# Attention probabilities turned by transposing DMAs through HBM for 22 of 32 head pairs, with weighings and loads in new places

## The reference, cut to what matters

```
Q = einsum('btc,ncd->btnd', x, W_Q) + b_Q      # and K, V; Q and K are then rotated (rope)
scores = einsum('bqnd,bknd->bnqk', Q, K) / math.sqrt(d_head)
scores = where(causal, scores, -inf)
probs = softmax(scores, axis=-1)
z = einsum('bnqk,bknd->bqnd', probs, V)
out = einsum('bqnd,ndm->bqm', z, W_O) + b_O
```

## Time and profile before

| | us |
|---|---|
| median of 3 runs | 954.27 (952.92 to 955.51) |
| the profiled execution: its time | 953.62 |
| the profiled execution: its span | 951.8 |
| TensorE busy | 911.5 |
| VectorE busy | 778.2 |
| GpSimd busy | 503.2 |
| ScalarE busy | 438.8 |

### The profile page before, as it was taken

One profiled execution on the slowest core, in us unless ns is written; L12 is line 12 of the kernel. 1 busy time (PEld: TensorE's weight loads), 2 busy tenths in 40 slices (PEclk: granted clock), 3 DMA queues, 4 the chain that ended last, 5 costly groups with the idle time before them and its releaser, 6 DMA issues.

```text
span 951.8 us, 19467 instructions
## 1 busy us (share of the span) xinstructions
PE 911.5 (96%) x6305; PEld 818.4 (86%) x6305; DVE 778.2 (82%) x1704; ACT 438.8 (46%) x1227; POOL 503.2 (53%) x380
## 2 busy tenths in 40 slices
PE   7899999999999999999999999989998799999996
PEld 6798888989899888998888888877887699999985
DVE  6988877977887999877799877767779688888867
ACT  3656655454334663333564333462156244444431
POOL 1433424465453436776354677525617377777760
PEclk9999999999999999999999999999999899999999
DMA  7796399899157952303793221315151277777768
GB/s 270 252 364 227 131 320 389 313 395 362 46 182 250 401 208 89 112 25 123 292 370 113 91 110 55 120 62 237 60 209 69 69 130 127 131 130 127 134 115 311
DMA packets 75584, 179.08 MB, mean 188 GB/s; under 512 B 7776, under 2 KB 42464, under 8 KB 74464
## 3 DMA queue, kind: packets, MB, share of 16 engines
q1 hardware_dynamic: 61040, 158.80, 46.0%
q0 software_dynamic: 14448, 19.05, 12.1%
HBM read 98.35 MB, written 79.47 MB: 187 GB/s over the span
## 4 chain that ended last, share of the span: by engine, by line
PE 80%; DVE 7%; issue 5%; POOL 3%; ACT 2%; DMA 1%; SPq 0%; DVEq 0%; ACTq 0%
PE bank L550 11%; PE bank L552 10%; PE bank L551 10%; PE bank L854 6%; PE bank L632 6%; PE bank L956 4%; POOL xs L1352 3%; PE bank L832 3%; PE bank L834 3%; PE bank L836 3%; PE bank L618 3%; PE bank L658 3%; PE bank L660 3%; PE bank L659 3%; PE bank L914 2%
## 5 line engine op out<-in xcount | busy, mean ns | idle before, releaser
L1312 POOL TENSOR_TENSOR z_lo<-prob_t,z_hi 128x512 fp32r<-128x512 f32 x64 | 82.5, 1297 | 188.5 <-ACT z_hi L1199 169.4
L1516 DVE SCALAR_TENSOR_TENSOR turn<-bank,bqk,trig 128x1024 f32<-128x1024 f32 x128 | 160.6, 1276 | 23.3 <-PE bank L552 20.8
L1344 POOL TENSOR_TENSOR rot<-turn 128x512 f32<-128x512 f32 x64 | 96.0, 1500 | 110.0 <-DVE turn L1516 94.6
L1405 POOL DMA_INDIRECT sums<-ysb,token_at x79 | 123.3, 1561 | 56.6 <-DMA sums<-ysb,token_at 28.0
L550 PE MATMUL bank<-xt_hi,w_hi 128*128 128x512 f32 x256 | 105.7, 413 | 3.4 <-DVE xt_lo L1480 1.7
L1185 ACT COPY prob_t<-bank 128x512 f32<-128x512 f32 x64 | 37.5, 586 | 148.8 <-PE bank L618 142.1
L1144 ACT ACTIVATE prob<-prob,negmax 128x128 f32<-128x128 f32 x256 | 99.1, 389 | 2.5 <-DVE negmax L1501 2.4
L552 PE MATMUL bank<-xt_hi,w_lo 128*128 128x512 f32 x256 | 100.1, 391 | 0.0
L551 PE MATMUL bank<-xt_lo,w_hi 128*128 128x512 f32 x256 | 99.7, 390 | 0.0
L1352 POOL DMA_INDIRECT xs<-xh,dest x64 | 74.3, 1161 | 41.2 <-issue 37.4
L1155 ACT COPY v<-bank 128x512 f32<-128x512 f32 x64 | 37.6, 587 | 114.5 <-PE bank L552 113.5
(11 more groups left out here) (197 smaller groups left out, 2643.3 us busy)
## 6 DMA issues: line engine op xcount, KB each, us to landing
xs<-zeros SPq DMA_DIRECT2D x16, 2120.0 KB, 15.3
w_hi<-w_dram SPq DMA_DIRECT2D x24, 768.0 KB, 9.7
w_lo<-w_dram SPq DMA_DIRECT2D x24, 768.0 KB, 9.1
xe_all<-xs SPq DMA_DIRECT2D x79, 132.5 KB
wo_hi<-wo_dram SPq DMA_DIRECT2D x26, 256.0 KB, 9.1
wo_lo<-wo_dram SPq DMA_DIRECT2D x26, 256.0 KB, 10.1
sums<-zeros SPq DMA_DIRECT2D x3, 2176.0 KB, 12.8
raw<-in_wqkv SPq DMA_DIRECT2D x16, 384.0 KB, 4.5
```

The lines of the kernel that those rows point to most:

```text
L1344: nc.gpsimd.tensor_tensor(rot[m][1][:], turn[m][1], turn[m][2], ALU.add).then_inc(rot_pool, 1)
L1405: nc.gpsimd.indirect_dma_start(sums_dram[s % SUMS], bass.IndirectOffsetOnAxis(ap=token_at[:, s:s + 1], axis=0), ysb[s % YBUFS][:], None, c ...
L1516: last = nc.vector.scalar_tensor_tensor(turn_all[m][:, 2 * i:2 * i + 2, :], qk_bank[2 * m + i][:].unsqueeze(1).to_broadcast([128, 2, GT]), ...
```

## The change

For the pairs t = 8 to 29 (`by_dma(t)`), which are weighed in steps 10 to 31, TensorE no longer turns the probabilities. ScalarE splits each head's fp32 probabilities into two planes of 16 bits (`prob_planes`), SP stores the planes to HBM (`prob_store`, 256 KB in rows of 256 bytes), waits for that store, and a transposing DMA brings them back as `prob_t` (`prob_turn`, 256 KB). The copies L1185 of these pairs are gone too. The other ten pairs stay as they were.

In these steps the weighings move: head 0 is weighed after projection QE (after the scores where p is 0 or 3), head 1 after KE. The loads of the weights go one pair ahead and stand between stores and turns on SP, and the zero fills and the fills of `sums` get other steps. On ScalarE the exponentials of head 0 now stand ahead of the taking of weighing 0, those of head 1 between the two; on VectorE the scaling of head 1's probabilities stands ahead of the two `rot`; on GpSimd the scaling of head 0's stands ahead of both `rot`, and `z_lo` of head 1 between them. At p = 1 and 2 both halves of the values come first. The turns of the mixer's output (p = 0) and the router's turns and logits (p = 2) move within their steps. Six semaphores are merged into others, which leaves their waits where they were.

```diff
@@ -69,8 +69,20 @@
 PARTS_DOWN = EXPERTS // GB
 
 
-FILL_STEPS = ([(1, p) for p in range(4)] + [(1, p) for p in (4, 4, 5, 5, 6, 6, 7)] + [(2, 3)]
-              + [(2, 3)] + [(GROUPS - 1, p) for p in (2, 3, 3)])
+FILL_STEPS = ([(1, p) for p in (0, 0, 1, 1)] + [(1, p) for p in (2, 3, 4, 4)] + [(1, p) for p in (5, 5, 6, 6)]
+              + [(1, 7)] + [(2, p) for p in (1, 2, 3)])
+
+
+def by_dma(t):
+    return PAIRS <= t < PAIRS * GROUPS - 2
+
+
+def dma_before(t):
+    return min(max(t - PAIRS, 0), PAIRS * (GROUPS - 1) - 2)
+
+
+def pe_before(t):
+    return t - dma_before(t)
...
+            def prob_store(t, h):
+                sp.wait_ge(planes_ready, 2 * dma_before(t) + h + 1)
+                rows = prob_dram[t % 2, h].rearrange("(b q i) k -> q b i k", b=GB, i=2)
+                sp.dma_start(rows, planes[h][:]).then_inc(prob_stored, 16)
+
+            def prob_turn(t, h):
+                sp.wait_ge(prob_stored, 16 * (2 * dma_before(t) + h + 1))
+                sp.wait_ge(z_lo_done, 2 * (t - 1) + h + 1)
+                sp.dma_start_transpose(prob_t[h][:].rearrange("p b q -> p (b q)").unsqueeze(1).bitcast(U16),
+                                       prob_dram[t % 2, h]).then_inc(prob_landed[h], 16)
+
...
             for g in range(1, GROUPS):
                 for p in range(PAIRS):
-                    at = W_AT[p]
-                    if g == 1 and W_NTH[p] == 0:
-                        sp.wait_ge(w_stored[at], 64 * W_USES[at])
-                    sp.wait_ge(v_ready, 2 * (PAIRS * (g - 1) + W_BEFORE[p] + 1))
-                    sp.wait_ge(wo_done, PAIRS * (g - 1) + W_BEFORE[p] - 1)
+                    t = g * PAIRS + p - 2
+                    if by_dma(t):
+                        prob_store(t, 0)
+                    if 0 < p < PAIRS - 1:
+                        load_w(g, p + 1)
+                    if by_dma(t):
+                        prob_turn(t, 0)
+                        prob_store(t, 1)
+                    if 0 < p < PAIRS - 1:
+                        load_o(g, p + 1)
+                    if by_dma(t):
+                        prob_turn(t, 1)
+                    if p == 0:
+                        load_w(g, 1)
+                        load_o(g, 1)
+                    if p == PAIRS - 1 and g < GROUPS - 1:
+                        load_w(g + 1, 0)
+                        load_o(g + 1, 0)
                     if g > 1 and p == 3:
                         sp.wait_ge(y_taken, FILTERS * (g - 1))
                         sp.dma_start(c_t[:], ctxt_in[g - 1]).then_inc(ctxt_loaded, 16)
-                    sp.dma_start(w_hi[:, at].bitcast(F32), w_dram[p, 0]).then_inc(w_loaded[at], 16)
-                    sp.dma_start(w_lo[:, at].bitcast(F32), w_dram[p, 1]).then_inc(w_loaded[at], 16)
-                    load_wo(p)
                     for n, at_step in enumerate(FILL_STEPS):
                         if at_step == (g, p):
                             fill(n // PARTS, n % PARTS)
...
 
             def weigh_values(s, p, h, first):
 
-                pe.wait_ge(pt_taken, s * 2 - 4 + h + 1)
+                t = s - 2
+                if by_dma(t):
+                    pe.wait_ge(prob_landed[h], 16 * (dma_before(t) + 1))
+                    if h == 0:
+                        pe.wait_ge(v_taken, s * 2 - 2)
+                else:
+                    pe.wait_ge(pt_taken, 2 * pe_before(t) + h + 1)
                 if not (first and p == 2 and h == 0):
                     pe.wait_ge(zt_taken, s * 2 - 4 + h)
...
+                h = g - 1
+                if p == 2 and 1 < g < GROUPS:
+                    two_banks_free(g, p, live)
+                    pe.wait_ge(v_taken, s * 2 - 1)
+                    token_turn(h - 1)
...
+                if p == 0 and 1 < g < GROUPS:
+                    two_banks_free(g, p, live)
+                    pe.wait_ge(v_taken, s * 2 - 1)
+                    cross_back(h - 1)
                 beside_first(g, p, live)
-                if live(2):
+                by_pe = live(2) and not by_dma(s - 2)
+                if by_pe:
                     transpose_probs(s, 0, live, order)
...
-                if live(2):
+                if by_pe:
                     transpose_probs(s, 1, live, order)
                     weigh_values(s, p, 0, first)
                     between_weighings(g, p, live)
@@ -864,6 +924,13 @@
                     if live(1) and order == (1, 0):
                         project_values(0)
                     weigh_values(s, p, 1, first)
+                elif live(2):
+                    between_weighings(g, p, live)
+                    if p in (0, 3):
+                        weigh_values(s, p, 0, first)
+                    if p == 2 and g > 1:
+                        pe.wait_ge(v_taken, s * 2)
+                        token_logits(g - 2, pt_bank)
                 beside_second(g, p, live)
...
                         project(p, col, qk_bank[i][:]).then_inc(qk_ready, 1)
-                if p == 2 and g > 1 and live(0):
-                    pe.wait_ge(zt_taken, s * 2 - 2)
-                    token_logits(g - 2, zt_bank)
+                    if live(2) and not by_pe and i == 0 and p not in (0, 3):
+                        weigh_values(s, p, 0, first)
+                    if live(2) and not by_pe and i == 2:
+                        weigh_values(s, p, 1, first)
...
+            def prob_planes(t, h):
+                act.wait_ge(prob_ready[h], t + 1)
+                if dma_before(t):
+                    act.wait_ge(prob_stored, 16 * (2 * dma_before(t) + h - 1))
+                nc.scalar.copy(planes[h][:], prob[h][:].bitcast(U16).rearrange("p b (k i) -> p b i k", i=2)).then_inc(planes_ready, 1)
...
+                if by_dma(s - 2):
+                    prob_planes(s - 2, 1)
...
+                if by_dma(s - 2):
+                    if p == 3:
+                        take_turned(v_t, g - 1, vt_ready, vt_taken)
+                    for h in range(2):
+                        exps(h)
+                        take_weighed(h)
+                        weighed_high(h)
+                elif live(2):
...
-                if live(1):
+                if live(1) and not by_dma(s - 2):
                     exps(0)
                     exps(1)
+                if by_dma(s - 1):
+                    prob_planes(s - 1, 0)
...
             def core_step(g, p, live, first):
                 s = g * PAIRS + p
+                late = by_dma(s - 2)
                 if live(2):
-                    z_low(g, p, live)
+                    z_low(s, 0)
+                    if not late:
+                        z_low(s, 1)
+                if late:
+                    first_probs(s)
                 for m in range(2):
+                    if late and m:
+                        z_low(s, 1)
                     if live(0):
                         pool.wait_ge(qk_used, s * 4 + 2 * m + 2)
                         if live(1):
                             pool.wait_ge(s_ready, s * 2)
                         pool_rot(m, s)
-                    if m == 0 and live(1):
-
-                        pool.wait_ge(rtotal_ready, s * 2 - 1)
-                        nc.gpsimd.tensor_tensor(prob[0][:], prob[0][:],
-                                                rtotal[:, 0, :].unsqueeze(2).to_broadcast([128, GB, SEQ]),
-                                                ALU.mult).then_inc(prob_ready[0], 1)
...
-                        if h == 1 and live(2):
-                            dve.wait_ge(pt_ready, s * 2 - 2)
+                        if by_dma(s - 2):
+                            dve.wait_ge(planes_ready, 2 * dma_before(s - 2) + h + 1)
...
+                def second_probs():
+                    dve.wait_ge(rtotal_ready, s * 2)
+                    nc.vector.tensor_tensor(prob[1][:], prob[1][:],
+                                            rtotal[:, 1, :].unsqueeze(2).to_broadcast([128, GB, SEQ]),
+                                            ALU.mult).then_inc(prob_ready[1], 1)
+
+                if by_dma(s - 1):
+                    second_probs()
...
-                if live(1):
-                    dve.wait_ge(rtotal_ready, s * 2)
-                    nc.vector.tensor_tensor(prob[1][:], prob[1][:],
-                                            rtotal[:, 1, :].unsqueeze(2).to_broadcast([128, GB, SEQ]),
-                                            ALU.mult).then_inc(prob_ready[1], 1)
+                if live(1) and not by_dma(s - 1):
...
                         tokens_low(h - 1)
+                    if p == 0:
+                        cross_add(h - 1)
                     if p == 3:
...
             def beside_scored(g, p, live):
                 h = g - 1
-                if p == 0 and h > 0:
+                if p == 2 and h > 0 and live(0):
+                    logits_take(h - 1, pt_bank)
+                if p == 0 and g == GROUPS:
```

134 lines of the change are left out of this document (74 added, 60 removed).

## The result

The changed kernel takes **959.75 us**, median of 20 runs (955.57 to 966.96), beside 955.85 us for the kernel before (20 runs): ratio 1.0045, interval 1.0025 to 1.0065. In a later series of runs the same two kernels stood at 960.34 and 951.00: ratio 1.0123 (1.0089 to 1.0157). The forecast was 6 us faster; it is slower, by 0.5% or by 1.2%. The profiled execution took 957.1 us.

A forecast was written before the change was run, and what follows sets the result against it. TensorE was taken to bound the kernel; turns removed and old waits gone, less new waits, late turns and 3.3 us for fills, gave 6.0 us off the profiled 953.62: 947.6, as a median 948; range 934 to 980.

The forecast's parts named there:

- Steps with p = 4 to 7: Twelve steps where a wait replaces the turns: 21.2 us against 21.44, 3 us gained for the twelve.
- The wait that takes the turns' place: Filter 4 waits 1.0 us for VectorE's product of filter 2, until S + 3.6; S ends the scores' issue.
- old waits for ScalarE: A weighing's waits for ScalarE's taking of the one before, 3.2 us; 2.3 of it was to go.
- the double fills: Steps 12 to 14 issue two fills each; turn 1 lands late in steps 14 and 15, 3.3 us lost.
- rival (c): Filter 4 doesn't wait, VectorE's product coming by S + 2.6: 1.0 us more in 12 steps, 936; chance 0.11.
- Steps with p = 0 to 3: Ten steps without that filter: the turns' 1.02 us come off each, less new waits for ScalarE and late turns.
- At p = 0 no loads stand between (free): At p = 0 the turns land in time, costing nothing; 2 x 1.0 us gained.
- x: Data time of one transposing DMA: taken as 1.2 us, bounds 0.75 and 3.4; turn 0 lands T + 8.5 + x, T the step's start.
- Rival (a): Transposing DMA slow, both weighings wait: at x = 3.4, 38 us more, 986; decides from x = 1.6; chance 0.28.
- likeliest case: The sum as worked out, x from 0.75 to 1.45: 944 to 952 us, chance 0.42.
- VectorE ... 3.5 us ahead: Scaling of head 1 (1.55 us) ahead of `rot` costs nothing: `rot` ended 3.5 us before the scores, 1.4 cover stays.
- Rival (b): Transposing DMA goes block by block, x = 16.4, every step bound by it: about 1,550 us; chance 0.06.

The follow-up runs named there:

- the last experiment: Changed kernel, turned by DMA only in the twelve steps with p = 4 to 7, weighing 0 there between filters 3 and 4: 948.21 us, 0.9964.
- the side-by-side runs: Unaltered changed kernel beside it with step 15's fill moved to step 31, and the kernel before: 960.34 us (1.0123), 953.79 (1.0035), 951.00.

## Why the prediction was wrong

**Steps with p = 4 to 7: the mechanism right, the sum near by luck.** The wait that takes the turns' place, its releaser, S + 3.5 and 21.3 us were as forecast. The twelve steps came out at -1.5 us, forecast -2.0, but by two errors that offset each other. Of the 5.3 us of gains (3.0 and 2.3) only some 2.4 came: step 22 with its 21.44 us was taken for all, while steps 12 to 15 had taken 21.21 before and so gained nothing, and of the 3.2 us of old waits for ScalarE only 1.1 lay in these steps, 1.8 with one that the trace puts down to "issue" (0.87 lay ahead of step 10, 1.26 behind step 31). And of the 3.3 us that the double fills were to lose only 0.9 came, in step 14. What rival (c) would be worth the last experiment shows: without that wait a step takes 20.5 us.

**Steps with p = 0 to 3: wrong, and the sign with them.** Forecast 4.0 us less, measured 7.4 more. The steps of the working that failed:

1. *"At p = 0 no loads stand between (free)" and "The fills ... 3.3 in all".* The queue was followed to step 15's own turns and not to the store of step 16, ahead of which stood step 15's loads for the next group and its fill. p = 0 missed by 4.7 us: step 16 by 5.6, while step 24 came out 1.0 better than forecast. Shown: with that one fill elsewhere step 16 falls by 5.1 us and the kernel is 0.9% faster, and the same fills without stores cost nothing that shows.
2. *"I take 1.2" for x, and 4.5 us for the loads.* x is 1.3 to 1.6 us in a quiet queue, not 1.2 (20 ns for a packet of 256 bytes where 16 were taken), and more where the turn runs into the end of loads: half of the 44 turns took over 1.6 us and eleven over 2, 2.3 in step 10, 2.8 at most, which the text had named as a sign of being wrong. The loads of 1.5 MB took 5.7 us in step 10, not 4.5 (4.7 to 7.2 over steps 10 to 31). In step 10 weighing 0 started at T + 11.4 and weighing 1 at T + 16.4, forecast 9.7 and 13.5 for their turns; the p = 1 steps and step 10 together missed by 2.1 us. Rival (a) gave x = 1.6 as the point from which it decides, and that is where the middle of the 44 turns lies (1.66). x lies between the bounds of 0.75 and 3.4 but for the most part above the 0.75 to 1.45 of the likeliest case.
3. *"VectorE ... 3.5 us ahead", costing nothing.* That cover was read in step 22 and taken for all. In steps 10 and 18 the scores now wait for `rot` (0.95 and 1.16 us; the waits for `rot` that the text had named as a sign of being wrong), and steps 18 and 26 missed by 1.7 us; at p = 3 the second projection of step 19 waits for VectorE (1.9 us), and turn 0 was late besides, in step 27 by 2.4, which missed 2.8. The run without turns keeps the wait for `rot` in step 10 and has that for `vcs` in both steps 19 and 27 (1.9 us each), so the turns are not their cause. The wait for `rot` in step 18 is gone there, and in the second execution of the changed kernel too, so that one comes and goes. What share the scaling's new place, the logits' new place and slower rots have was not separated.
4. *Not in the sum at all: the clock.* The text priced a wait at its length. Of the 10.9 us of the side-by-side runs up to 5.5 are low clock. In the profile of the kernel before, steps 10 to 31 have none. Waits do not all bring it: in two profiled executions of the changed kernel it fell after those of 3.48 and 3.41 us in step 16 and 3.04 in step 27; after 2.0 to 2.7 us it fell sometimes (2.03 in step 19 of the second execution, yes, in the row below; 2.41 in step 27 of the first and 2.73 in step 10 with the fill moved, no).

```profile
355.80:359.30 3.50, 3.50 (x10) 1.95 (x8) 3.17 (x6) 2.15 (x9) 0.00 (x0) 0.51 0.48 121
```

**The rules of the Trainium skill's pages.** Rival (b), blocks one by one, is out: a whole head is turned in about 1.5 us of DMA time, not ten. So the 1309 ns for one block in the Trainium skill's page "VectorE: DVE Perf Modes", section "The three transpose paths", do not add up over eight blocks here; that page's rule, TensorE where PSUM will do, still came out right for the ten steps with p = 0 to 3. What the Trainium skill's page "Advanced Engine Details and Errata", section "X-Bar Transpose (TRN2)", says, that transposing DMAs are as fast as regular ones, the trace bears out only roughly, and in a quiet queue only: 1.3 to 1.6 us for a turn against 1.0 to 1.2 for the store of the same bytes.

**What stays open.** In the run without turns the profile gains 5.6 us in steps 10 to 31 and the medians about 1. The two profiles are of different series, and between these the kernel before itself moved, from 955.85 to 950.8 us; it was profiled in the first alone. Within the series the mean clock, 0.9915 against 0.9926, is worth 1.0 us of the rest. And what stands behind step 31 took 346.4 us before, 347.9 without turns, 349.4 in the last experiment (whose steps gain 7.4 us and whose median gains 3.4; it opens with a wait of 2.44 us for `z_lo`) and 342.7 to 349.4 over the profiles at hand (nearly the same code in all). How much of a gain in the steps is given back there, and why, was not found. Nor was it settled why the changed kernel lost 0.5% in one series and 1.2% in another.

## What to carry to other kernels

Where a small transfer on the critical path shares a queue with large ones, write down what stands ahead of it at every step boundary, the step after a fill too, and do not answer with a queue of its own before measuring: packets of 256 bytes beside packets of 4 KB were four times slower than behind them, and their DMA six. TensorE paid for new waits of 2.0 to 3.5 us once as idle time and often again as half clock, so work taken off a full TensorE has to be worth more than its waits look. And look for cover in the fullest step of the other engines, not in a typical one: the turns paid only in the four of eight steps in which they were not waited for, and there only once the work of a weighing filled the wait for VectorE that they had left behind. Last, a row read in one step stands for its kind only after the other steps have been read too: step 22 stood for twelve steps and for VectorE's cover, and both times wrongly.

## What the runs showed of the hardware that was not expected

- A turn of a head (256 KB read, 1024 packets of 256 bytes) takes 1.3 to 1.6 us of data time in a quiet queue and up to 2.8 among the ends of loads in its own. Two beside loads and a fill on another queue took 17.8 us, beside loads alone 9.3 and 11.3, and with nothing beside them 3.8.
- SyncE is held 1.16 us by the issue of a transposing DMA, against mostly 0.39 to 0.58 for a store, and for up to 2.06 us in some of the 44.
- The store's rows went out as 512 packets of 512 bytes, mostly 26 to 30 ns each, not as 1024 of 256.
- VectorE's `rot` took 1562 ns by the mean of steps 10 to 31 instead of 1221, and the scaling of head 1 1090 instead of 1455, after the two changed places. In the changed kernel a `rot` took 0.68 us with no instruction of GpSimd beside it and 1.55 us or more with one beside it in all but one case; in the kernel before half of them took 0.66 us beside one, so that GpSimd is the cause is not shown.
